# W's Strassen sums formed in PSUM by TensorE, unit by unit, instead of on VectorE and GpSimd

## The reference

```python
y      = einsum('bct,bcd->bdt', x, w[idx])               # per sample, 128 x 2048
result = einsum('bnd,od->bno', y, W_base) + b_base       # W_base is 2048 x 2048
probs  = softmax(einsum('bnd,ed->bne', y, W_gate))       # 8 experts, the best 2 are kept
route  = top 2 of probs, scaled to sum 1
delta  = einsum('bner,eor->bno', (y @ A) * route, B)     # rank 16 per expert
out    = x + result + delta
```

## Time and profile before

| | us |
|---|---|
| median of 3 runs | 1632.52 |
| lowest and highest of them | 1632.2, 1632.76 |
| the profiled execution's own time | 1634.34 |
| its span in the trace | 1632.6 |
| granted TensorE clock, mean of the span | 0.972 |
| busy: PE | 1536.8 (94%) |
| busy: DVE | 1300.2 (80%) |
| busy: POOL | 631.9 (39%) |
| busy: ACT | 596.5 (37%) |

### The profile page before, as it was taken

How to read it: one execution, slowest core, us unless ns; L and a number is a source line. 1 busy time by engine, 2 the same in 40 slices (tenths; PEclk the granted TensorE clock), 3 DMA queues, 4 the chain that set the end, 5 groups by cost and what they waited for, 6 DMA issues and landing times.

```text
span 1632.6 us, 25730 instructions
## 1 busy us (share of the span) xinstructions
PE 1536.8 (94%) x9539; PEld 837.8 (51%) x9539; DVE 1300.2 (80%) x2228; ACT 596.5 (37%) x996; POOL 631.9 (39%) x473
## 2 busy tenths in 40 slices
PE   5667999999999999999668999999999999999998
PEld 5444555555555555555464555555555555555553
DVE  6666888888888888888776888888888888888874
ACT  6654333333333333333583323333322333332231
POOL 2534455555555555555453122222212221221222
PEclk8788999999999999999889999999999999999999
DMA  5332444444444444444731344343334434333432
GB/s 198 130 117 82 128 136 136 135 135 134 128 136 136 136 127 133 132 134 125 235 104 39 98 137 136 110 122 121 102 91 136 136 113 121 122 105 88 134 107 71
DMA packets 102911, 201.87 MB, mean 124 GB/s; under 512 B 10874, under 2 KB 24186, under 8 KB 102266
## 3 DMA queue, kind: packets, MB, share of 16 engines
q1 hardware_dynamic: 102786, 200.22, 39.8%
HBM read 128.96 MB, written 71.22 MB: 123 GB/s over the span
## 4 chain that ended last, share of the span: by engine, by line
PE 89%; DVE 5%; ACT 2%; issue 2%; DMA 1%; POOL 1%; POOLq 0%; SPq 0%; DVEq 0%; ACTq 0%
PE bank_x L1121 10%; PE bank_x L1122 10%; PE bank_x L1123 10%; PE bank_y L1123 10%; PE bank_y L1122 10%; PE bank_y L1121 10%; PE bank_z L1121 3%; PE bank_z L1123 3%; PE bank_z L1122 3%; PE bank_h L1122 3%; PE bank_h L1121 3%; PE bank_h L1123 3%; PE bank_c L1121 2%; PE bank_c L1123 2%; PE bank_c L1122 2%
## 5 line engine op out<-in xcount | busy, mean ns | idle before, releaser
L475 POOL TENSOR_TENSOR x_res<-x_res,t_sums 128x512 f32<-128x512 f32 x256 | 350.7, 1372 | 895.6 <-DVE t_sums L827 735.5
L1121 PE MATMUL bank_x<-TT,s_parts 128*128 128x512 f16 x768 | 295.5, 385 | 14.8 <-POOL TT L450 7.5
L1122 PE MATMUL bank_x<-TT,s_parts 128*128 128x512 f16 x768 | 295.0, 384 | 0.0
L1123 PE MATMUL bank_x<-TT,s_parts 128*128 128x512 f16 x768 | 294.6, 384 | 0.0
L1121 PE MATMUL bank_y<-TT,s_parts 128*128 128x512 f16 x768 | 291.2, 379 | 0.0
L1122 PE MATMUL bank_y<-TT,s_parts 128*128 128x512 f16 x768 | 291.1, 379 | 0.0
L1123 PE MATMUL bank_y<-TT,s_parts 128*128 128x512 f16 x768 | 291.1, 379 | 0.0
L571 ACT ACTIVATE p_copies<-bank_x,y_inv 128x512 f32<-128x512 f32 x128 | 87.8, 686 | 492.8 <-PE bank_x L1123 398.7
L827 DVE TENSOR_TENSOR t_sums<-t_sums,inv_w 128x512 f32<-128x512 f32 x256 | 218.6, 854 | 8.8
L800 DVE TENSOR_TENSOR s_parts<-a_full,s_parts 128x512 f16<-128x512 f32 x224 | 208.1, 951 | 7.5 <-ACT s_parts L556 7.5
L456 POOL TENSOR_TENSOR x_res<-x_res,BT 128x512 f32<-128x512 f32 x128 | 197.8, 1545 | 4.8 <-DMA x_res<-in_x_dram 3.3
(11 more groups left out here) (219 smaller groups left out, 2715.6 us busy)
## 6 DMA issues: line engine op xcount, KB each, us to landing
x<-in_x_dram SPq DMA_DIRECT2D x32, 1024.0 KB, 5.7
x_res<-in_x_dram SPq DMA_DIRECT2D x128, 256.0 KB, 3.7
part_scratch<-x_res SPq DMA_DIRECT2D x128, 256.0 KB, 2.9
x_res<-part_scratch SPq DMA_DIRECT2D x128, 256.0 KB, 3.9
out_dram<-x_res SPq DMA_DIRECT2D x128, 256.0 KB, 2.8
x_parts<-in_L_ffn_W_base_dram SPq DMA_DIRECT2D x12, 512.0 KB, 5.3
a_full<-in_L_ffn_W_base_dram SPq DMA_DIRECT2D x12, 512.0 KB, 4.8
w_cond<-in_L_cond_weights_dram SPq DMA_DIRECT2D x64, 64.0 KB, 3.9
```

Of the source, the lines that this page charges most:

```text
L475: nc.gpsimd.tensor_tensor(XR[:, xr_slot(m), :], XR[:, xr_slot(m), :], TM[:, m % 2, :], ALU.add).then_inc(r_added, 1)
L1121: nc.tensor.matmul(dst, lhs[0], rhs[0], start=start, stop=False, skip_group_check=chained)
L1122: nc.tensor.matmul(dst, lhs[0], rhs[1], start=False, stop=False, skip_group_check=chained)
L1123: return nc.tensor.matmul(dst, lhs[1], rhs[0], start=False, stop=stop, skip_group_check=chained)
```

## The change

Three things change in the preparation of W; the products, the activations and the output path stay as they are.

1. **TensorE adds the sums in PSUM.** A unit is now 7 quads in two chains. One bank holds in turn B11, then B11 - C12 (which is -T1), then T2, then T4: each stage adds a transposed block, with a diagonal of plus or minus the scale, to what the bank holds. Another bank holds B22, then T3, and then, started afresh, B21. After each stage ACT takes the upper part from the bank and DVE the lower part (`w_lower(g, q)`, now DVE's), and only then may PE add the next stage. Two units are interleaved in a period: B11(g), B22(g), T2(g-1), spread(g), B21(g-1), T1(g), T4(g-1), T3(g). ACT and DVE follow that order. The copy of C12, the four sums of DVE, the four roundings of ACT and the four lower parts of POOL are gone.
2. **The scales.** ACT sums the first row block only; DVE sums the second with a reduction of 128 x 1024. The diagonals are made by POOL (`w_diagonals`): two of plus the scale, two of minus the scale, two inverses.
3. **Rows.** The units of the middle take three row buffers in turn, and unit g's rows are loaded once T4 of unit g-3 has been added. In the opening the rows of unit 2 are loaded at once, and the later loads and tile loads are placed anew on SP. `transpose_maxima(1)` and `spread_maxima(1)` stand ahead of `product(0, 0, 0)` and `product(0, 0, 1)`, since units 4 to 7 now use the bank in which they write. `find_maxima(1)` stays where it is in DVE's order.

`n_stage(g, q)` numbers the stages in the order in which they are done. The diff, cut to its core (the opening of PE, ACT and DVE is rearranged in the same way as the parts shown):

```diff
+        ROOT, SIDE = 0, 1
+        CHAIN = {B11: ROOT, T1: ROOT, T2: ROOT, T4: ROOT, B22: SIDE, T3: SIDE, B21: SIDE}
...
+        def bank_of(g, q):
             if NU // 2 <= g < NU:
-                return (BX[1], BD)[i % 2]
-            if g < NU // 2:
-                return (BX[0], BX[1], BY[0], BY[1])[i]
-            return (BX[0], BX[1], BY[0], BY[1], BZ)[(4 * (g % NU) + i) % 5]
-
-
-        xr_rows = XR[:, :, :].rearrange("p (s t) n -> p s (t n)", t=2)
+                return ((BX[1], BD), (BC, BY[0]))[CHAIN[q]][g % 2]
+            return (BX, BY)[CHAIN[q]][g % 2]
...
+        RESIDUAL, BIAS, COPIES, PARTS, FREE, FULL = range(6)
+        AREA = [RESIDUAL, BIAS, COPIES, RESIDUAL, PARTS, FREE, FULL, PARTS,
+                PARTS, FULL, COPIES, PARTS, FULL, COPIES, PARTS, FULL]
...
             sp.wait_ge(cond_done, 4)
+            load_rows(4)
+            sp.wait_ge(w_tr, n_stage(3, T4))
             load_rows(5)
+            for m in range(2, 4):
+                load_tile(m)
             sp.wait_ge(s_lo, NPROD)
-            load_rows(4)
+            load_rows(6)
...
+                    sp.wait_ge(r_added, 8 * NP)
+                    load_rows(NU + 2)
...
-                    for g in range(NU + 2, 2 * NU):
-                        sp.wait_ge(w_tr, 4 * (g - 1))
+                    for g in range(NU + 3, 2 * NU):
+                        sp.wait_ge(w_tr, n_stage(g - 3, T4))
                         load_rows(g)
...
-            def w_lower(g):
-                u = g % NU
-                for i, q in enumerate((T1, T3, T2, T4)):
-                    pool.wait_ge(w_sum_hi, 4 * g + i + 1)
-                    nc.gpsimd.tensor_tensor(t_dst(q, u, 1), quads(t_full(g, q)), t_dst(q, u, 0),
-                                            ALU.subtract).then_inc(w_sum_lo, 1)
+            def w_diagonals(g):
+
+                pool.wait_ge(w_scaled, g + 1)
+                if g > 1:
+                    pool.wait_ge(w_tr, n_stage(g - 2, T4))
+                for i in range(2):
+                    ins = nc.gpsimd.tensor_scalar(diag[g % 2][:, i, :], ident[:, :], row_rpow2[:, g % 2, i:i + 1], TOP_W,
+                                                  ALU.mult, ALU.mult)
+                ins.then_inc(w_diag, 1)
+                if g > 0:
+                    pool.wait_ge(w_spread, g)
+                for i in range(2):
+                    nc.gpsimd.tensor_scalar(minus_diag(g)[:, i, :], ident[:, :], row_rpow2[:, g % 2, i:i + 1], -TOP_W,
+                                            ALU.mult, ALU.mult)
+                    ins = nc.gpsimd.tensor_scalar(diag_inv[:, i, :], ident[:, :], row_pow2[:, g % 2, i:i + 1],
+                                                  1.0 / TOP_W, ALU.mult, ALU.mult)
+                ins.then_inc(w_minus, 1)
...
+                act.wait_ge(rows_in[AREA[g]][0], row_turn(g))
+                if g == NU:
+                    act.wait_ge(prod_done, n_prod(NP - 1, 1, NPROD - 1))
+                nc.scalar.activation(TT[:, B22, u // 4, :, :, u % 4 * P:(u % 4 + 1) * P],
+                                     rows_of(g, 0).rearrange("p a (c n) -> p a c n", c=C4), ACT.Abs,
+                                     accum_out=row_sum[:, g % 2, 0:1]).then_inc(w_sums, 1)
...
+            def w_upper(g, q):
+                act.wait_ge(w_tr, n_stage(g, q))
...
+                nc.scalar.activation(t_dst(q, g % NU, 0), quads(bank_of(g, q)[:, :]), ACT.Copy,
+                                     scale=-1.0 if q == T1 else 1.0).then_inc(w_hi, 1)
...
+            def w_period(g):
+                w_inverse(g)
+                w_upper(g, B11)
+                w_upper(g, B22)
+                w_upper(g - 1, T2)
+                w_upper(g - 1, B21)
+                w_upper(g, T1)
+                w_upper(g - 1, T4)
+                w_upper(g, T3)
...
+                    sum_rows(NU + 1)
+                    w_begin(NU)
+                    for g in range(NU + 1, 2 * NU):
                         if g + 1 < 2 * NU:
                             sum_rows(g + 1)
-                        w_upper(g)
-                    act.wait_ge(w_sum_lo, 4 * 2 * NU)
+                        w_period(g)
+                    w_end(2 * NU - 1)
...
             def w_scales(g):
+                dve.wait_ge(rows_in[AREA[g]][1], row_turn(g))
+                link(nc.vector.tensor_reduce(row_sum[:, g % 2, 1:2], rows_of(g, 1), AX_XY, ALU.add,
+                                             apply_absolute_value=True))
...
-                for i in range(2):
-                    nc.vector.tensor_scalar(diag[g % 2][:, i, :], ident[:, :], row_rpow2[:, i:i + 1], TOP_W,
-                                            ALU.mult, ALU.mult)
-                    ins = nc.vector.tensor_scalar(diag_inv[:, i, :], ident[:, :], row_pow2[:, i:i + 1], 1.0 / TOP_W,
-                                                  ALU.mult, ALU.mult)
-                ins.then_inc(w_diag, 1)
...
+                    dve.wait_ge(w_minus, g - 1)
+                power_of_two(row_pow2[:, g % 2, :], row_sum[:, g % 2, :], row_clamped[:, :])
+                nc.vector.reciprocal(row_rpow2[:, g % 2, :], row_pow2[:, g % 2, :]).then_inc(w_scaled, 1)
...
+            def w_lower(g, q):
+                dve.wait_ge(w_hi, n_stage(g, q))
+                nc.vector.scalar_tensor_tensor(out=t_dst(q, g % NU, 1), in0=quads(bank_of(g, q)[:, :]),
+                                               scalar=-1.0 if q == T1 else 1.0, in1=t_dst(q, g % NU, 0),
+                                               op0=ALU.mult, op1=ALU.subtract).then_inc(w_lo, 1)
...
             w_scales(4)
+            find_top(1)
             features(0)
+            scale_x(1)
             finish(0, 0, C11)
-            find_top(1)
             w_scales(5)
-            w_sums_and_lower(4)
+            w_begin(4)
+            w_scales(6)
+            w_period(5)
             finish(0, 0, C12)
-            w_scales(6)
-            w_sums_and_lower(5)
+            w_scales(7)
+            w_period(6)
             finish(0, 0, C21)
             finish(0, 0, C22)
-            w_scales(7)
-            w_sums_and_lower(6)
-            w_sums_and_lower(7)
-            scale_x(1)
+            w_period(7)
+            w_end(7)
...
+            def w_quad(g, q):
...
+                if q == B11:
+                    pe.wait_ge(w_diag, g + 1)
+                    if g - 2 >= begin:
+                        pe.wait_ge(w_lo, n_stage(g - 2, T4))
...
+                elif q == B21:
+                    pe.wait_ge(w_lo, n_stage(g, T3))
+                    block_of, half, scale = 0, 1, plus
+                elif q == T1:
+                    pe.wait_ge(w_minus, g + 1)
+                    pe.wait_ge(w_lo, n_stage(g, B11))
+                    block_of, half, scale = 1, 0, minus
+                elif q == T3:
+                    pe.wait_ge(w_lo, n_stage(g, B22))
+                    block_of, half, scale = 1, 0, minus
+                elif q == T2:
+                    pe.wait_ge(w_lo, n_stage(g, T1))
+                    block_of, half, scale = 1, 1, plus
+                else:
+                    pe.wait_ge(w_lo, n_stage(g, T2))
+                    block_of, half, scale = 0, 1, minus
+                opens = q in (B11, B22, B21)
...
+                    mm = nc.tensor.matmul(bank_of(g, q)[:, c * P:(c + 1) * P], rows[:, half, c * P:(c + 1) * P],
+                                          scale[block_of], start=opens and c == 0, stop=True, skip_group_check=True)
...
+            def w_period(g):
+                w_quad(g, B11)
+                w_quad(g, B22)
+                w_quad(g - 1, T2)
+                spread(g)
+                w_quad(g - 1, B21)
+                w_quad(g, T1)
+                w_quad(g - 1, T4)
+                w_quad(g, T3)
...
+            transpose_maxima(1)
+            pe.wait_ge(w_lo, n_stage(NU // 2 - 1, T4))
             pe.wait_ge(a_copied, 4)
             product(0, 0, 0)
```

More of the change, by code:

```diff
@@ new lines, in adaln_ffn_kernel, with phase_of, n_stage @@
+        CHAIN = {B11: ROOT, T1: ROOT, T2: ROOT, T4: ROOT, B22: SIDE, T3: SIDE, B21: SIDE}
+        def phase_of(g):
+            return (0, NU // 2 - 1) if g < NU // 2 else (NU // 2, NU - 1) if g < NU else (NU, 2 * NU - 1)
+        def bank_of(g, q):
+            if NU // 2 <= g < NU:
+                return ((BX[1], BD), (BC, BY[0]))[CHAIN[q]][g % 2]
+            return (BX, BY)[CHAIN[q]][g % 2]
+        def n_stage(g, q):
+            begin, end = phase_of(g)
+            v = g - begin
+            if q in (B11, B22, T1, T3):
+                if v == 0:
+                    return 7 * begin + (B11, B22, T1, T3).index(q) + 1
+                return 7 * (begin + v - 1) + 4 + {B11: 1, B22: 2, T1: 5, T3: 7}[q]
+            if g == end:
+                return 7 * end + 4 + (T2, B21, T4).index(q) + 1
+            return 7 * g + 4 + {T2: 3, B21: 4, T4: 6}[q]
@@ L186, in adaln_ffn_kernel @@
         wc_in = sem("wc_in")
-        stage_in = [sem(f"stage{i}_in") for i in range(4)]
```

(46 more changed lines are left out.)

307 lines of the change are left out of this document (139 added, 168 removed).

## The result

The changed kernel took **1659.95 us** (median of 4 runs, 1659.06 to 1660.4), the kernel before 1632.64 in the same session: a ratio of **1.0166**, interval 1.0149 to 1.0184. The direction was as forecast, the amount not: +27.3 us against a forecast of +9.4, outside the range.

The account below looks back on a forecast made before the run. Bound by PE except in W's preparation, where a round trip ACT to DVE to ACT sets the units. Opening -1.2, middle's order +7.8 and clock +2.8 sum to +9.4 on 1632.52: 1641.9 us, range 1628 to 1651.

Parts of the forecast that it names:

- P = D + 4.7 with D = 5.2: 9.9 us: Middle: a unit's period P, with the row transfer exposed and the second block landing D after issue; 9.9 against 7.83 us.
- quads begin 0.6 after 800.96 [...] the first T4 at 813.5: Middle's start, before the five periods: two quads at the low clock, then T1 at 805.4 and the first T4 ending 813.5.
- the tail: Middle's end, after the five periods: remaining quads from T3 to the last T4 and its lower part, 12.5 us.
- 2.8 for the clock: Middle: low clock after PE's idle time assumed in two of five periods, +2.8 us, ends 0 and 7.
- 875.5: Middle: time the preparation ends, 813.5 + 5 x 9.9 + 12.5; with a product of 2.6, +7.8 us.
- ACT [...] loses, by my estimate, some 2 to the rounds through PSUM [...] end 63.2, 2.3 later: Opening, units 0 to 3: chain starts at 54.1, four rounds of 2.3, last lower part ends 63.2 instead of 60.88.
- PE's waits of 9.4 behind a work of 48.4 in the opening: Opening: from PE's start at 80.4, work plus waits on lower parts put half 1's first product at 138.2; -1.2 us.
- +5 if quads run at the low clock: Opening: upper end of the -1.2 us term, should its quads run at the low clock.
- The transfer is hidden: Rival, middle: second block lands early, P falls to 6.9, no low clock, -8.4 us, 1624.1; chance 0.15.
- The clock stays low in every period: Rival, middle: all five periods at the low level, +4.2 more, 1646.1, or 1651 with the opening's quads; chance 0.2.
- The diagonals are slow on POOL: Rival: diagonals of 0.57 cost +2 in the first four units; at 1.15 each +4 in all, 1646; chance 0.05.
- The parts cancel: Rival: D = 4.3, P = 9.0, no low clock, opening's waits overlap to -4; no change, 1631.8; chance 0.1.

Follow-up runs that it names:

- The load a quad later: Changed kernel with the loads of units 11 to 15 released by the quad after T4, one quad later; 1670.6 us, ratio 1.0226 to the kernel before.
- the moved sums: Changed kernel with, in the middle, the row sums and scales of unit g+1 moved behind B21(g-1); 1655.73 us, ratio 1.0133 to the kernel before.
- the run with the output copies later: Changed kernel with DVE's scales of unit 7 and lower parts of the opening's last units ahead of half 1's output copies; 1650.66 us.
- the run with the clock held: Changed kernel plus 40 matmuls of ones on PE between step 15 and unit 8, result unchanged; 1657.43 us, ratio 1.0144 to the kernel before.
- the run with the maxima behind the products: Changed kernel with sums, inverse copy, maxima and output copies reordered, plus half 1's maxima transposed and spread behind the first two products; 1628.02 us.
- the last two kernels: Changed kernel with all four moves and maxima behind products, without and with 40 added matmuls of ones in the middle; 1628.02 and 1625.0 us.

## Why the prediction was wrong in size

Of the error, 9.0 us lie in the opening (+7.8 against -1.2) and 8.1 in the middle (+18.7 against +10.6). The period was right; three terms around it failed.

**The period held.** "P = D + 4.7 with D = 5.2: 9.9 us" measured 10.14 to 10.35 at the high clock. The waits are those forecast: DVE 3.06 and ACT 2.56 for a DMA, PE 2.4 ahead of T1. The load a quad later, and the moved sums, show that the transfer is what binds. Four of the five periods together with their clock cost 42.32, against 39.6.

**"quads begin 0.6 after 800.96 [...] the first T4 at 813.5" failed**: 5.9 too early (27.2 against 21.3 from step 15's last product). I let T1(8) follow the two quads at once and had B11's eviction 0.6 after its quad. ACT's inverse copy, which I had counted in its sum of work (the 0.25), stood ahead of that eviction and waited for the spread. Moving it gave 5.0 back in the middle. The same omission made the tail 14.3 (879.45 to 893.79) in place of 12.5: 1.8 more. In the run with the copy moved the tail is 13.0. With 3.1 for five periods (52.6 against 49.5; 2.8 for the clock had been put aside for them) the middle's excess of 10.8 over 875.5 is complete.

**"ACT [...] loses, by my estimate, some 2 to the rounds through PSUM [...] end 63.2, 2.3 later" failed**: 6.1 later. This term I had estimated rather than walked through, and the same inverse copy lay in it: with the copy moved, the first product started 3.0 sooner, of the 3.8 that the last lower part was behind the forecast. Together with the maxima (forecast 80.0, measured 82.2) it made the first product 2.1 late.

**PE's waits of 9.4 behind a work of 48.4 in the opening failed: the waits were too small and the clock behind them was left out.** The waits ahead of T1(6) and T1(7) were forecast for the right reason, 3.0 and 2.6, and measured 4.21 and 3.27: 1.9 more. After each the quads were at the low level, four from 122.37 to 128.86 and three from 137.67 to 142.11, which by the distances of their starts is some 4.6 us more than at 0.9 each. I had named that as an end, "+5 if quads run at the low clock", and not put it in the sum, although show 2.08 after only 2.06 idle, and the trace of the kernel before has a product at the low level (starts 0.43 apart, not 0.22) behind a wait of 2.87 too:

```profile
107.62 1.21 PE L1150 MATMUL bank_d<-diag,x_parts 128*128 128x128 f32 x8 [2.87 <-DVE TT L936]
108.62 0.63 PE L1121 MATMUL bank_x<-TT,s_parts 128*128 128x512 f16 x1
```

2.1 + 1.9 + 4.6 = 8.6 of the 8.95 by which half 1's first product was late. The run with the output copies later, which takes both waits away, starts it 6.8 sooner.

**The rivals.** "The transfer is hidden" claims that P then falls to 6.9. No run hides the transfer in the old order, but the last unit, which waits for no rows, gives an estimate: B11(15) to T1(15) takes 4.8 (880.95 to 885.76), by the inverse copy, and T1 to the next B11 3.8 (877.18 to 880.95), 8.6 in all. In the other order of the experiments P was 9.5, by the inverse copy, and 8.4 with that moved too, by DVE's scales. "The clock stays low in every period" did not hold: 1.00 at 840:860, with PE idle 2.4 to 2.6 in each period. "The diagonals are slow on POOL" did not: 0.37 each and 0.82 for the first pair, hidden. "The parts cancel" asked for the second block 4.3 after its issue; DVE had it at 5.3, and the opening's waits grew.

The Trainium skill ("TensorE: Matmul & The Clock Gate", section "A second HAM failure mode: psum-queue depth-cycling") would have the low level come back among such short pauses. The trace of the changed kernel disagrees for its steady periods; the run with the clock held agrees (0.91 at 820:840, with a pause of 2.98; 0.83 at 860:880, with pauses of 2.12 and 2.74). What was wrong with my use of it was the place. In the five periods, for which 2.8 was put in the sum, the low level cost some 1.3 (the first of them, 11.55 against 10.14 to 10.35); in the opening, for which nothing was, 4.6.

## What to carry to other kernels

Where an order written by hand is changed, walk every wait of every engine in the new order, small copies too: an operation of 0.37 us cost 8.2 us, because it waited in front of work that was ready, and part of that was the lower clock behind the waits. Two waits that lie behind each other show little when one alone is removed (4.1 and 5.0) and much when both are (16.5). And a change that adds up to a loss can lose by its orders alone: with them mended, the kernel with the PSUM sums is 0.3 to 0.55% faster than the kernel before. That the sums themselves are the gain does not follow, since the kernel before kept its own orders.

## What the hardware showed that was not expected

A small operation of DVE can last as long as POOL's operation beside it. In the run with the maxima behind the products, POOL and DVE:

```profile
76.61 2.25 POOL L495 TENSOR_TENSOR TT<-TT 128x1088 f16<-128x1088 f32 x1
```

```profile
75.42 1.20 DVE L966 TENSOR_REDUCE row_sum<-x_parts 128x1 f32<-128x1024 f32 x1
76.65 2.23 DVE L807 TENSOR_SCALAR row_clamped<-row_sum 128x2 f32<-128x2 f32 x1
```

Two columns take 0.17 elsewhere and 2.23 here: both end at 78.9. DVE's next small operation does so again (1.14 from 78.92, POOL's next ends at 80.04). The reduction ran beside POOL's operations at its usual 1.20. The Trainium skill ("SBUF — State Buffer", section "Who interferes with whom") tells of a pair of ports that DVE and GpSimd hold one at a time, for a whole instruction; the trace agrees, with the operation of 2.23 as long as POOL's remainder. In the changed kernel this cost 1.0 at 120.25, ahead of T1(6).

The clock of a stretch differs between executions of the same instructions. Up to step 15 the last two kernels are the same code; the first line is of the one without the added matmuls, the second of the one with them:

```profile
80.00:100.00 20.00, 19.39 (x143) 15.47 (x142) 13.76 (x30) 8.96 (x17) 11.78 (x23) 1.00 0.35 127
```

```profile
80.00:100.00 20.00, 19.93 (x155) 15.93 (x156) 12.40 (x29) 6.00 (x13) 9.44 (x16) 0.91 0.45 157
```

At 60:80 they were granted 0.91 and 0.83, and half 1 started 5.4 us apart, 1.3 of which stood already at 60 us (0.83 and 0.74 at 20:40). The kernel before has no such spread (1631.7 to 1635.0 in 13 runs, against 1622.9 to 1630.7 in 9). A difference of 0.2% between such kernels is not to be read from one execution of each.
